# Column halves in the values' product, attention on the memory rows first, and a new order of steps, in a two-layer cross-attention kernel

## The chip, the cores and the metric

The kernel runs on one core of a Trainium2 chip, as one launch. The metric is the device time of that launch in microseconds (us). TensorE (PE), VectorE (DVE), ScalarE (ACT), GpSimd (POOL) and SyncE (SP, which here only starts transfers) work side by side and wait for each other on semaphores. All data is float32. "PEld" is TensorE's loading of stationary operands, which the profile lists apart from its products.

## The reference, cut to what matters

There are 32 sequences of 64 tokens with 256 features. Layer 0 is an expert block: each token goes through one of two weight sets ("v" and "l"). Layer 1 attends to a memory of 64 rows with 128 features for each sequence.

```python
# layer 0 (16 heads; head width 16 in self-attention, 8 in cross-attention)
x = rms_norm(hidden, ln_in_w)
q, k, v = split(where(vm, x @ v_qkv, x @ l_qkv))
ctx = softmax(causal(rope(q) @ rope(k).T / 4)) @ v
hidden = hidden + where(vm, ctx @ v_dense, ctx @ l_dense)
ck, cv = split(encoder @ ckv_w)
cctx = softmax(rms_norm(hidden) @ cq_w @ ck.T / sqrt(8)) @ cv
hidden = hidden + cctx @ cdense_w
mi = rms_norm(hidden)
hidden = hidden + where(vm, silu(mi@v_gate)*(mi@v_up)@v_down, silu(mi@l_gate)*(mi@l_up)@l_down)

# layer 1 (one head, width 256; W_mem is 256 x 128)
memory_proj = memory @ W_mem.T
attn = softmax(hidden @ memory_proj.T / 16)
memory_context = attn @ memory_proj
gate = sigmoid(concat(hidden, memory_context) @ W_gate.T + b_gate)
out = rmsnorm(hidden + gate * memory_context) * norm_w
```

## The kernel before

The 2048 tokens are 16 tiles of 128 tokens; a tile holds two sequences (b = 0 and 1, 64 rows each). Two tiles (t = 0 and 1) make a group, and there are 8 groups. A tile goes through steps with names: `qkv`, `qkvv` (projections), `qkT` (turn queries and keys), `score_a`/`score` (scores), `probT` (turn the exponentials), `pv` (weights times values), `ctxT`, `dense`, `h1T`, `cproj`, and then the same for cross-attention: `cscore_a`/`cscore`, `cprobT`, `cpv`, `cctxT`, `cdense`. The finished rows are scattered to DRAM in the order of their expert (`sort`). The third part, the expert MLP, works on 17 slots m of 128 sorted rows: `m_in`, `miT`, `gu0` to `gu2`, `hT0`, `hT1`, `down`, `m_out`. Layer 1 (section L1 of the order) gathers the rows back (`h3_in`) and runs `h3T`, `hw`, `mscore`, `attnT`, `gate`, `fuse`, `fin`, `store` for each of the 16 tiles, with four sets of buffers u.

The order in which each engine does its steps is written out by hand in a table `ORDER`, one list for each engine and section: W0 to W7 (a group of layer 0 each, from W1 on with MLP slots mixed in), MID (the rest of the MLP) and L1. `run` walks through the table. An engine never leaves this order, it only waits.

Precise products split both operands in a high and a low part (`split_product`, `x_product`). A plain float32 product of the kernel shows up in the trace as two matmul records, each with a weight load of its own; a turn (`transpose`) shows up as one.

Scores are computed in strips: the stationary operand is 32 rows by 64 columns, so that a quarter of the array's rows and half of its columns work on one strip, and four strips (`strip_scores`, line 1344) with different rows lie in the array side by side. The mask is put in by a product with 64 rows (line 1353). Everything else in layer 0 uses all 128 rows and columns.

The values' product is `apply` (line 1381), called by `pv` (hd = 16) and `cpv` (hd = 8). For each of 8 pairs of heads, the stationary operand is `pT[t][:, k, :]`: 128 rows (two heads by 64 keys) by 128 columns (two sequences by 64 queries). The moving operand holds the values of both sequences, 2 x 2 x (hd + 1) columns, 68 or 36 wide; the one more column gives the sum of the exponentials. So every query gets a result with the values of both sequences, and `normed` (lines 1034 and 1038, on DVE) reads only the half that belongs to it: two reciprocals and two multiplications, one for each sequence, each on 64 partitions.

In layer 1, `h3T` turns the tile's rows (line 1536) and computes `mp` = memory @ W_mem.T (line 1539, 256 columns); ACT copies both at once (line 786, 512 columns). `mscore` computes the scores (lines 1561 and 1562) and, into the other half of the bank, `mpg` = memory @ (W_gate2 @ W_mem).T (line 1563, 256 columns); ACT copies it (line 800) after the exponentials (line 799). `attnT` turns the weights (line 1569; copy in line 805), and `gate` multiplies them with `mp` (line 1574) and with `mpg` (line 1575).

## Time and profile before

| | us |
|---|---|
| median of 3 runs | 557.07 (554.66 to 559.98) |
| the profiled execution, its own time | 557.75 |
| its span, first to last instruction | 555.9 |
| busy in the span: PE / PEld / DVE | 482.8 / 389.9 / 380.2 |
| busy in the span: ACT / POOL | 252.5 / 150.5 |
| mean granted TensorE clock | 0.959 of full |

The busy times overlap, since engines work side by side. The span has four stretches: start and group W0 up to about 85 us, where weights are still loaded and split; six repeats of the same 50.3 us (W1 to W6) up to 386 us; W7 and MID up to about 465 us; and layer 1 from 470 us to the end. Between MID and layer 1 TensorE waits for rows that go to DRAM and come back.

### The profile page before, as it was taken

How to read it: one execution, taken by the hardware profiler on the slowest of the kernel's cores; microseconds unless marked ns; L12 is line 12 of the kernel's file. 1: busy time of each engine (PE TensorE's matmuls, PEld its weight loads, DVE VectorE, ACT ScalarE, POOL GpSimd, SP SyncE). 2: the span in 40 equal slices, each digit the busy share in tenths (PEclk: the TensorE clock that was granted, in tenths of full speed). 3: DMA queues.
4: the chain of work that ended last, by engine and by line, in shares of the span. 5: the costliest groups of instructions: out<-in, count | busy, mean ns of one | idle time of the engine just before them, and what ended most of it. 6: DMA issues, size and time to landing. Idle time of an engine off the chain costs nothing.

```text
span 555.9 us, 9884 instructions
## 1 busy us (share of the span) xinstructions
PE 482.8 (87%) x3462; PEld 389.9 (70%) x3462; DVE 380.2 (68%) x852; ACT 252.5 (45%) x694; POOL 150.5 (27%) x262
## 2 busy tenths in 40 slices
PE   0688887999999999999999999999997895988984
PEld 0566465677778777877878787777776784856762
DVE  4889978876885888588578858875875452245444
ACT  3256434444544445355354525443542331555663
POOL 6162221213031230303131221313011202254452
PEclk9978799999999999999999999999998798888998
DMA  6643500001011000101010110001000131021111
GB/s 202 186 132 102 171 10 20 11 29 58 2 39 47 22 11 28 59 11 39 11 58 2 40 47 21 19 20 50 1 11 22 36 106 47 11 75 54 43 58 38
DMA packets 22688, 27.07 MB, mean 49 GB/s; under 512 B 3280, under 2 KB 19408, under 8 KB 22640
## 3 DMA queue, kind: packets, MB, share of 16 engines
q1 hardware_dynamic: 20992, 22.08, 12.6%
q0 software_dynamic: 1648, 4.36, 2.6%
q8 instruction: 29, 0.48, 0.3%
q14 instruction: 19, 0.16, 0.1%
HBM read 19.74 MB, written 6.68 MB: 48 GB/s over the span
## 4 chain that ended last, share of the span: by engine, by line
PE 71%; DVE 16%; ACT 6%; DMA 3%; issue 3%; SPq 1%; POOL 1%; POOLq 0%; ACTq 0%
PE xyz L1318 8%; PE xyz L1344 7%; PE b_ps L1497 7%; PE xyz L1381 5%; PE xyz L1322 4%; PE xyz L1369 3%; DVE E L1018 3%; PE b_ps L1500 3%; DVE mx L1016 3%; PE xyz L1547 2%; PE b_ps L1289 2%; PE b_ps L1290 2%; PE b_ps L1291 2%; PE b_ps L1511 2%; ACT vb L685 2%
## 5 line engine op out<-in xcount | busy, mean ns | idle before, releaser
L1195 POOL TENSOR_TENSOR var<-ss,pow_eps 128x1 f32<-128x1 f32 x32 | 8.2, 256 | 247.7 <-ACT att L664 164.7
L1381 PEld LDWEIGHTS xyz<-vb,kT 128*128 128x128 f32 x512 | 62.1, 196 | 7.2 <-issue 5.4
L1381 PE MATMUL xyz<-vb,kT 128*128 128x36 f32 (+1 forms) x512 | 63.5, 280 | 1.5 <-DVE kT L1071 1.2
L1016 DVE TENSOR_REDUCE mx<-xyz 128x8 f32<-128x512 f32 x64 | 43.7, 683 | 11.5 <-PE xyz L1344 11.4
L1344 PE MATMUL xyz<-kT,qT 32*64 32x128 f32 (+1 forms) x768 | 44.4, 332 | 4.9 <-ACT qT L722 3.3
L1369 PE MATMUL xyz<-cst,E 128*128 128x128 f32 x256 | 39.2, 287 | 8.3 <-ACT E L695 5.6
L1018 DVE TENSOR_TENSOR E<-xyz,mx 128x512 f32<-128x512 f32 x64 | 44.2, 691 | 2.2
L1369 PEld LDWEIGHTS xyz<-cst,E 128*128 128x128 f32 x256 | 29.5, 146 | 14.9 <-ACT E L695 8.3
L1497 PE MATMUL b_ps<-w_gu_hi,ms_hi 128*128 (+2 forms) x90 | 37.4, 416 | 0.6 <-ACT ms_hi L752 0.6
L728 ACT ACTIVATE E<-E,rstd 128x512 f32<-128x512 f32 x32 | 23.1, 723 | 31.2 <-DVE E L1018 31.2
L1344 PEld LDWEIGHTS xyz<-kT,qT 32*64 32x64 f32 x768 | 21.0, 135 | 20.9 <-PE xyz L1344 8.4
L685 ACT ACTIVATE vb<-xyz,rstd 64x128 f32<-64x128 f32 x64 | 23.6, 369 | 26.5 <-PE xyz L1322 25.3
L1497 PE MATMUL b_ps<-w_gu_lo,ms_hi 128*128 (+2 forms) x90 | 34.1, 380 | 0.0
L695 ACT ACTIVATE E<-E 128x512 f32<-128x512 f32 x32 | 20.1, 628 | 28.6 <-DVE E L1018 28.6
L1289 PE MATMUL b_ps<-w_down_hi,hidT_hi 128*128 (+1 forms) x90 | 27.4, 304 | 1.2 <-DVE hidT_lo L1115 1.2
L764 ACT ACTIVATE th<-b_ps,mrh 128x256 f32<-128x256 f32 (+1 forms) x45 | 20.0, 444 | 17.5 <-PE b_ps L1500 17.3
L1500 PE MATMUL b_ps<-w_gu_hi,ms_lo 128*128 (+2 forms) x90 | 26.9, 381 | 0.0
L1318 PE MATMUL xyz<-w_qkv_hi,xs_vhi 128*128 128x512 f32 (+1 forms) x64 | 23.6, 380 | 2.9 <-issue 2.3
L1290 PE MATMUL b_ps<-w_down_lo,hidT_hi 128*128 (+1 forms) x90 | 26.2, 291 | 0.0
L1291 PE MATMUL b_ps<-w_down_hi,hidT_lo 128*128 (+1 forms) x90 | 26.1, 290 | 0.0
L1122 DVE TENSOR_TENSOR xm<-b_ps,xm 128x256 f32<-128x256 f32 x15 | 6.4, 425 | 27.7 <-PE b_ps L1291 27.6
L1097 DVE SCALAR_TENSOR_TENSOR th<-th,b_ps 128x256 f32<-128x256 f32 (+1 forms) x45 | 17.6, 391 | 10.5 <-ACT th L764 9.3
(268 smaller groups left out, 1305.0 us busy)
## 6 DMA issues: line engine op xcount, KB each, us to landing
xm<-h_rows SPq DMA_DIRECT2D x17, 128.0 KB, 2.1
h_rows<-xm SPq DMA_DIRECT2D x17, 128.0 KB, 1.7
xT<-in_xT_dram SPq DMA_DIRECT2D x8, 256.0 KB, 3.1
x_sb<-in_x_dram SPq DMA_DIRECT2D x8, 256.0 KB, 3.1
ctxT_a<-in_ctxT_dram SPq DMA_DIRECT2D x8, 128.0 KB, 2.3
over_xs<-in_ctxT_dram SPq DMA_DIRECT2D x4, 256.0 KB, 3.3
out_dram<-late SPq DMA_DIRECT2D x8, 128.0 KB, 1.7
out_dram<-over_qkv SPq DMA_DIRECT2D x8, 128.0 KB, 1.7
```

The costliest lines, as they stand in the source:

```text
L685: act.activation(vb[t][e * SEQ:(e + 1) * SEQ, b, :, e, 0:HD], v[rows, :, e, :], ACT.Copy, scale=rstd[rows, 0, t:t + 1]).then_inc(S["vb_rea ...
L1016: dve.tensor_reduce(mx[:, t, heads], s, AX.X, ALU.max).then_inc(max_ready, 1)
L1018: dve.tensor_tensor(E[t][:, b * 512:(b + 1) * 512].rearrange("p (h k) -> p h k", k=SEQ), s, mx[:, t, heads].unsqueeze(2).to_broadcast([P, ...
L1289: pe.matmul(o, sh, mh, start=start, stop=False)
L1290: pe.matmul(o, sh, ml, start=False, stop=False)
L1291: return pe.matmul(o, sl, mh, start=False, stop=stop)
L1318: pe.matmul(o, xs[e][0][:, c, cols], w_qkv[s][:, e, c, a:b], start=(e == 0 and c == 0 and s == 0), stop=False)
L1344: last = pe.matmul(xy[t][q, hp, o:o + w], qT[t][rows, c, q], kT[t][rows, (2 * c + b) * w:(2 * c + b + 1) * w], start=not masked, stop=True ...
L1369: last = pe.transpose(xy[t][:, a // 4, (a % 4) * P:(a % 4 + 1) * P], E[t][:, a * P:(a + 1) * P], ident)
L1381: last = pe.matmul(yz[t][:, a, 0:4 * (hd + 1)], pT[t][:, k, :], vb[t][:, :, a, :, HD - hd:HD + 1], start=True, stop=True)
L1497: pe.matmul(o, ms[m % 2][0][:, c, :], weights(s, c), start=(c == 0 and s == 0), stop=False)
L1500: last = pe.matmul(o, ms[m % 2][1][:, c, :], weights(0, c), start=False, stop=(c == HC - 1))
```

## The change: what it does

In `apply` each product is made twice, once for each sequence b: the stationary operand is 128 rows by the 64 columns of b's queries, the moving operand has b's values alone (34 or 18 columns), and the result goes to b's 64 partitions. So there are 16 products where there were 8, each with half of the array's columns. `normed` then reads one layout on all 128 partitions: one reciprocal and one multiplication.

In layer 1, `h3T` turns the memory rows instead of computing `mp`; ACT copies 384 columns. `mpg`, its product and its copy are gone. A new step `mix` multiplies the turned memory rows with the attention weights (128 columns), ACT copies the result (`mixT`), and `gate` is one product with `w_memT`, 512 columns wide, which gives both halves.

`inv_rms` counts on one semaphore instead of two, which frees the semaphores for `mix`. Its instructions stay.

```diff
             def apply(t, hd, done):
                 for k in range(PAIRS):
                     a = 4 * (k % 4 // 2) + 2 * (k // 4) + k % 2 if hd == HD else k
-                    last = pe.matmul(yz[t][:, a, 0:4 * (hd + 1)], pT[t][:, k, :], vb[t][:, :, a, :, HD - hd:HD + 1], start=True, stop=True)
+                    for b in range(2):
+                        q = slice(b * SEQ, (b + 1) * SEQ)
+                        last = pe.matmul(yz[t][q, a, 0:2 * (hd + 1)], pT[t][:, k, q], vb[t][:, b, a, :, HD - hd:HD + 1], start=True, stop=True)
                 last.then_inc(done, 1)
...
             def normed(n, t, hd, pv_ps, rec_ready, done):
-                for b in range(2):
-                    rows = slice(b * SEQ, (b + 1) * SEQ)
-                    dve.reciprocal(rec[rows, t, :]..., o[rows, b, :, :, hd]).then_inc(rec_ready, 1)
-                for b in range(2):
...
-                    dve.tensor_tensor(att[t][rows, 0:NH * hd]..., o[rows, b, :, :, 0:hd], ... ALU.mult).then_inc(done, 1)
+                dve.reciprocal(rec[:, t, :].rearrange("p (a e) -> p a e", e=2), o[:, :, :, hd]).then_inc(rec_ready, 1)
+                dve.wait_ge(rec_ready, tl(n, t))
+                dve.tensor_tensor(att[t][:, 0:NH * hd]..., o[:, :, :, 0:hd], ... ALU.mult).then_inc(done, 1)
...
             def h3T_(n, t):        # TensorE
-                pe.matmul(L[u][:, H:2 * H], memory(n, t), w_memT[:, 0:H], start=True, stop=True).then_inc(S["h3T_ps"], 1)
+                pe.transpose(L[u][:, H:H + P], memory(n, t), ident).then_inc(S["h3T_ps"], 1)
...
             def h3T_(n, t):        # ScalarE
-                act.activation(h3m[u], L[u], ACT.Copy).then_inc(S["h3T_ready"], 1)
+                act.activation(h3m[u][:, 0:H + P], L[u][:, 0:H + P], ACT.Copy).then_inc(S["h3T_ready"], 1)
...
             def mscore(n, t):      # TensorE, and its copy on ScalarE
-                pe.matmul(L[u][:, 0:P], hwT[u], memory(n, t), start=False, stop=True)
-                pe.matmul(L[u][:, H:2 * H], memory(n, t), w_memT[:, H:2 * H], start=True, stop=True).then_inc(S["ms_ps"], 1)
+                pe.matmul(L[u][:, 0:P], hwT[u], memory(n, t), start=False, stop=True).then_inc(S["ms_ps"], 1)
-                act.activation(mpg[u], L[u][:, H:2 * H], ACT.Copy).then_inc(S["mpg_ready"], 1)
...
+            def mix(n, t):         # TensorE
+                pe.wait_ge(S["mwT_ready"], tl(n, t))
+                pe.matmul(L[u][:, 0:P], mem[u], mwT[u], start=True, stop=True).then_inc(S["mix_ps"], 1)
+            def mix(n, t):         # ScalarE
+                act.wait_ge(S["mix_ps"], tl(n, t))
+                act.activation(mixT[u], L[u][:, 0:P], ACT.Copy).then_inc(S["mix_ready"], 1)
             def gate(n, t):
-                pe.matmul(L[u][:, 0:H], mwT[u], mp[u], start=True, stop=True)
-                pe.matmul(L[u][:, H:2 * H], mwT[u], mpg[u], start=True, stop=True).then_inc(S["gate_ps"], 1)
+                pe.wait_ge(S["mix_ready"], tl(n, t))
+                pe.matmul(L[u], mixT[u], w_memT[:, :], start=True, stop=True).then_inc(S["gate_ps"], 1)
...
             ("W2", dict(           # the table ORDER, TensorE's list, one of all that are new
-                    miT:1 qkT:4 qkT:5 score_a:4 score:4 gu0:1 gu1:1 score_a:5 probT:4 score:5 gu2:1 pv:4 probT:5
+                    qkT:4 miT:1 qkT:5 score_a:4 score:4 gu0:1 gu1:1 score_a:5 probT:4 score:5 gu2:1 hT0:1 pv:4 probT:5
```

The table is new in every section. Three places show what that means. The first is TensorE in W2, from the values' product of tile 4 (`pv:4`) to that of tile 5; the name `kT` stands for `pT`, which shares its buffer. Before:

```order
L1381 MATMUL xyz<-vb,kT 128x68 x8
L1369 MATMUL xyz<-cst,E 128x128 x8
L1392 MATMUL xyz<-cst,att 128x128 x2
L1398 MATMUL xyz<-ctxT_a,w_ckv 128x128
L1399 MATMUL xyz<-w_ckv,ctxT_a 128x128
L1511 MATMUL b_ps<-cst,hid 128x128 x6
L1289 MATMUL xyz<-w_dense_hi,attT_hi 128x512
L1290 MATMUL xyz<-w_dense_lo,attT_hi 128x512
L1291 MATMUL xyz<-w_dense_hi,attT_lo 128x512
```

And after the change:

```order
L1514 MATMUL b_ps<-cst,hid 128x128 x4
L1384 MATMUL xyz<-vb,kT 64x34 x16
L1370 MATMUL xyz<-cst,E 128x128 x8
L1514 MATMUL b_ps<-cst,hid 128x128 x2
L1395 MATMUL xyz<-cst,att 128x128 x2
L1401 MATMUL xyz<-ctxT_a,w_ckv 128x128
L1402 MATMUL xyz<-w_ckv,ctxT_a 128x128
L1384 MATMUL xyz<-vb,kT 64x34 x16
```

The eight products are sixteen of half the size; two of the six turns of `hid` stand between the exponentials' turns and those of `att`; and `pv:5` follows `ctxT:4` at once, where `dense:4` stood between them before. The second place is DVE around the same two products. Before:

```order
L1034 RECIPROCAL rec<-xyz 64x16 x2
L1038 TENSOR_TENSOR att<-xyz,rec 64x256 x2
L1055 TENSOR_TENSOR attT_lo<-xyz,attT_hi 128x256
L247 TENSOR_TENSOR kT<-xyz,cst 128x512
L1026 COPY kT<-xyz 128x512
L1047 SCALAR_TENSOR_TENSOR h_0<-xyz,route_t,x_sb 128x256
L1050 SCALAR_TENSOR_TENSOR h_0<-xyz,route_t,h_0 128x256
```

And after the change:

```order
L1037 RECIPROCAL rec<-xyz 128x16
L1039 TENSOR_TENSOR att<-xyz,rec 128x256
L1031 COPY kT<-xyz 128x512
L1056 TENSOR_TENSOR attT_lo<-xyz,attT_hi 128x256
L247 TENSOR_TENSOR kT<-xyz,cst 128x512
L1037 RECIPROCAL rec<-xyz 128x16
L1039 TENSOR_TENSOR att<-xyz,rec 128x256
```

Each pair of instructions is one, and the second tile's copy and division come ahead of the first tile's residual sum. The third place is TensorE in layer 1, near the end, where the steps of several tiles alternate. Before:

```order
L1536 MATMUL xyz<-cst,over_qkv 128x128 x2
L1539 MATMUL xyz<-w_memT,over_xs 128x256
L1561 MATMUL xyz<-block_h,ident_h 128x128
L1562 MATMUL xyz<-over_xs,over_qkv 128x128
L1563 MATMUL xyz<-w_memT,over_xs 128x256
L1574 MATMUL xyz<-late 128x256
L1575 MATMUL xyz<-late 128x256
```

And after the change (1539 and 1542 are `h3T`, 1564 and 1565 `mscore`, 1575 `gate`, 1580 `mix`):

```order
L1575 MATMUL xyz<-w_memT,late 128x512
L1539 MATMUL xyz<-cst,over_qkv 128x128 x2
L1542 MATMUL xyz<-cst,over_xs 128x128
L1564 MATMUL xyz<-block_h,ident_h 128x128
L1565 MATMUL xyz<-over_xs,late 128x128
L1548 MATMUL xyz<-over_qkv,w_mem 128x128 x2
L1550 MATMUL xyz<-w_gate,over_qkv 128x256 x2
```

The two products with `w_memT` and 256 columns are gone from their places, a turn stands for the first, and the 512 columns are made at once in `gate`.

## Rows read from the trace of the kernel before

**Rows 1.** Busy time in stretches: length, then PE, PEld, DVE, ACT, POOL, clock, DMA.

```profile
0.00:84.80 84.80, 57.07 (x353) 43.26 (x354) 66.66 (x139) 36.50 (x78) 31.35 (x55) 0.90 0.43 132
135.10:185.40 50.30, 48.14 (x385) 39.73 (x384) 38.14 (x83) 23.33 (x63) 11.70 (x20) 1.00 0.10 30
470.00:545.00 75.00, 67.39 (x341) 52.69 (x342) 32.42 (x99) 43.03 (x148) 34.32 (x55) 0.91 0.16 48
```

**Rows 2.** The chain that ended last, by engine.

```profile
PE 71%; DVE 16%; ACT 6%; DMA 3%; issue 3%; SPq 1%; POOL 1%; POOLq 0%; ACTq 0%
```

**Rows 3.** PE in order of time (start, length, count): `pv`, turns of `cprobT`, `cpv`.

```profile
199.91 1.90 PE L1381 MATMUL xyz<-vb,kT 128*128 128x68 f32 x16
201.64 0.39 PE L1415 MATMUL xyz<-cst,h 128*128 128x128 f32 x2
...
211.81 1.04 PE L1369 MATMUL xyz<-cst,E 128*128 128x128 f32 x8
212.68 0.61 PE L1423 MATMUL xyz<-qT,w_cq 128*128 128x128 f32 x4
...
215.00 1.97 PE L1381 MATMUL xyz<-vb,kT 128*128 128x36 f32 x16
216.81 0.41 PE L1497 MATMUL b_ps<-w_gu_hi,ms_hi 128*128 x1
```

**Rows 4.** PEld, the loads of one `cscore` from 205.30 on: one, four, five.

```profile
205.30 0.13 PEld L1344 LDWEIGHTS xyz<-kT,qT 32*64 32x64 f32 x1
205.30 0.15 PEld L1344 LDWEIGHTS xyz<-kT,qT 32*64 32x64 f32 x4
205.30 0.19 PEld L1344 LDWEIGHTS xyz<-kT,qT 32*64 32x64 f32 x5
```

**Rows 5.** PEld by line and shape: count, busy us, mean ns, idle before.

```profile
L1381 PEld LDWEIGHTS xyz<-vb,kT 128*128 128x128 f32 x512 | 62.1, 196 | 7.2 <-issue 5.4 <-ACT kT L733 1.1
L1369 PEld LDWEIGHTS xyz<-cst,E 128*128 128x128 f32 x256 | 29.5, 146 | 14.9 <-ACT E L695 8.3 <-ACT E L728 5.3 <-issue 1.0
```

**Rows 6.** The chain in layer 1 in order of time: start, length, what.

```profile
482.57 0.45 PE xyz L1545 x4
...
518.29 0.43 PE xyz L1539 x2
...
519.06 0.43 PE xyz L1563 x2
...
523.82 0.43 PE xyz L1574 x2
```

**Rows 7.** PE in order of time around one half of the cross scores.

```profile
206.39 0.39 PE L1399 MATMUL xyz<-w_ckv,ctxT_a 128*128 128x128 f32 x2
206.71 0.66 PE L1344 MATMUL xyz<-kT,qT 32*64 32x256 f32 x8
207.30 0.50 PE L1497 MATMUL b_ps<-w_gu_hi,ms_hi 128*128 x1
207.64 0.40 PE L1497 MATMUL b_ps<-w_gu_lo,ms_hi 128*128 x1
```

**Rows 8.** DVE and PE by line and shape, around `normed`.

```profile
L1034 DVE RECIPROCAL rec<-xyz 64x16 f32<-64x16 f32 x64 | 16.1, 252 | 2.6 <-PE xyz L1381 1.5
L1038 DVE TENSOR_TENSOR att<-xyz,rec 64x256 f32<-64x256 f32 x32 | 13.5, 422 | 1.0
L1038 DVE TENSOR_TENSOR att<-xyz,rec 64x128 f32<-64x128 f32 x32 | 9.2, 289 | 1.0
L1392 PE MATMUL xyz<-cst,att 128*128 128x128 f32 x32 | 7.0, 301 | 2.4 <-DVE att L1038 2.1
```

**Rows 9.** ACT by line and shape in layer 1.

```profile
L786 ACT ACTIVATE late<-xyz 128x512 f32<-128x512 f32 x8 | 4.8, 596 | 12.5 <-PE xyz L1539 12.3
L791 ACT ACTIVATE late<-xyz 128x128 f32<-128x128 f32 x8 | 2.2, 278 | 6.1 <-PE xyz L1547 6.1
L800 ACT ACTIVATE late<-xyz 128x256 f32<-128x256 f32 x8 | 3.0, 377 | 0.0
```

More of the change, by code:

```diff
@@ L181, in xattn_kernel @@
         h3T = [h3m[u][:, 0:H].rearrange("p (c q) -> p c q", c=HC) for u in range(NB)]
-        mp = [h3m[u][:, H:2 * H] for u in range(NB)]
-        mpg = [late_piece(u, 3 * H, 4 * H) for u in range(NB)]
+        mem = [h3m[u][:, H:H + P] for u in range(NB)]
+        mixT = [h3m[u][:, H + P:H + 2 * P] for u in range(NB)]
         mw = [late_piece(u, 4 * H, 4 * H + P) for u in range(NB)]
@@ L366, in xattn_kernel @@
+                    cprobT:2 hT1:0 cscore:3 down:0 cpv:2 cprobT:3 cctxT:2 cdense:2 cpv:3 qkv:4 cctxT:3 cdense:3 qkvv:4
+                    qkv:5 qkvv:5""",
             )),
@@ L385, in xattn_kernel @@
+                    cscore:4 gu2:2 hT0:2 cproj:5 cscore_a:5 cprobT:4 hT1:2 cscore:5 down:2 cpv:4 cprobT:5 cctxT:4
+                    cdense:4 cpv:5 qkv:6 cctxT:5 cdense:5 qkvv:6 qkv:7 qkvv:7""",
             )),
@@ L404, in xattn_kernel @@
+                    cscore:6 gu2:4 hT0:4 cproj:7 cscore_a:7 cprobT:6 hT1:4 cscore:7 down:4 cpv:6 cprobT:7 cctxT:6
+                    cdense:6 cpv:7 qkv:8 cctxT:7 cdense:7 qkvv:8 qkv:9 qkvv:9""",
             )),
@@ L423, in xattn_kernel @@
+                    cscore:8 gu2:6 hT0:6 cproj:9 cscore_a:9 cprobT:8 hT1:6 cscore:9 down:6 cpv:8 cprobT:9 cctxT:8
+                    cdense:8 cpv:9 qkv:10 cctxT:9 cdense:9 qkvv:10 qkv:11 qkvv:11""",
             )),
@@ new lines, in xattn_kernel @@
+                    probT:11 hT1:7 ctxT:10 miT:8 ctxT:11 h1T:10 gu0:8 dense:10 cproj:10 gu1:8 h1T:11 dense:11 gu2:8
+                    hT0:8 cproj:11 cscore:10 cprobT:10 hT1:8 cscore:11 cprobT:11 cctxT:10 xsq:12 cctxT:11 xsq:13
+                    rope:12 rope:13""",
+                dve="""
+                    qkT:10 miT:7 qkT:11 score:10 gu0:7 gu1:7 probT:10 score:11 gu2:7 pv:10 probT:11 hT1:7 hT0:7
+                    ctxT:10 pv:11 miT:8 down:7 dense:10 ctxT:11 xsplit:12 dense:11 gu0:8 gu1:8 cscore:10 gu2:8 hT0:8
+                    cprobT:10 hT1:8 cscore:11 cpv:10 cprobT:11 cdense:10 cpv:11 xsq:12 down:8 cdense:11 xsq:13 rope:12
+                    rope:13""",
@@ L457, in xattn_kernel @@
-                    cscore:13 cpv:12 gu2:10 cprobT:13 hT0:10 cdense:12 hT1:10 xsq:14 cpv:13 down:10 cdense:13 xsq:15
-                    rope:14 rope:15""",
+                    qkT:12 miT:9 qkT:13 score:12 gu0:9 gu1:9 probT:12 score:13 gu2:9 pv:12 probT:13 hT1:9 hT0:9
+                    ctxT:12 pv:13 miT:10 down:9 dense:12 ctxT:13 xsplit:14 dense:13 gu0:10 gu1:10 cscore:12 gu2:10
+                    hT0:10 cprobT:12 hT1:10 cscore:13 cpv:12 cprobT:13 cdense:12 cpv:13 xsq:14 down:10 cdense:13
@@ new lines, in xattn_kernel @@
+                    mix:1 fuse:0 hw:3 attnT:2 gate:1 mscore:3 mix:2 fuse:1 attnT:3 mix:3 gate:2 h3T:4 fuse:2 hw:4
+                    gate:3 mscore:4 h3T:5 attnT:4 fuse:3 mix:4 hw:5 h3T:6 mscore:5 gate:4 attnT:5 hw:6 mix:5 fuse:4
+                    mscore:6 h3T:7 attnT:6 gate:5 hw:7 mix:6 fuse:5 mscore:7 attnT:7 gate:6 mix:7 fuse:6 h3T:8 gate:7
+                    hw:8 fuse:7 h3T:9 mscore:8 hw:9 attnT:8 mix:8 h3T:10 mscore:9 attnT:9 gate:8 hw:10 h3T:11 fuse:8
+                    mix:9 mscore:10 attnT:10 hw:11 mix:10 gate:9 mscore:11 attnT:11 fuse:9 gate:10 mix:11 h3T:12
@@ new lines, in xattn_kernel @@
+                    mix:1 hw:3 gate:1 attnT:2 mscore:3 mix:2 attnT:3 gate:2 mix:3 h3T:4 gate:3 hw:4 mscore:4 h3T:5
+                    attnT:4 hw:5 mix:4 h3T:6 gate:4 mscore:5 hw:6 attnT:5 mix:5 mscore:6 h3T:7 gate:5 attnT:6 hw:7
+                    mix:6 mscore:7 gate:6 attnT:7 h3T:8 mix:7 gate:7 hw:8 h3T:9 mscore:8 hw:9 attnT:8 h3T:10 mix:8
+                    mscore:9 gate:8 attnT:9 hw:10 h3T:11 mscore:10 mix:9 hw:11 attnT:10 gate:9 mix:10 mscore:11
+                    gate:10 attnT:11 mix:11 h3T:12 gate:11 hw:12 mscore:12 attnT:12 h3T:13 mix:12 hw:13 gate:12 h3T:14
@@ L539, in xattn_kernel @@
+                    mscore:13 hw:14 attnT:13 h3T:15 mscore:14 mix:13 hw:15 attnT:14 gate:13 mix:14 mscore:15 gate:14
+                    attnT:15 mix:15 gate:15""",
             )),
@@ L1224, in xsq @@
                     pool.wait_ge(S["vb_ready"], 4 * (tl(n, t) - 2))
-                inv_rms(0, t, n, S["ssx"], S["r1v"], S["r1"])
+                inv_rms(0, t, n, S["ssx"], S["r1"])
             def rope_add(n, t):
@@ L1233, in dense @@
             def dense(n, t):
-                inv_rms(1, t, n, S["ss1"], S["r2v"], S["r2"])
+                inv_rms(1, t, n, S["ss1"], S["r2"])
             def m_sq(n, t):
@@ L1389, in ctxT @@
             def ctxT(n, t):
-                pe.wait_ge(S["att_ready"], half(n, t, 1))
+                pe.wait_ge(S["att_ready"], tl(n, t))
                 for c in range(HC):
```

277 lines of the change are left out of this document (124 added, 153 removed).

## The prediction

> **What bounds the kernel now.** I read the stretches first. In a repeat of 50.30 us TensorE works 48.14 us at the full granted clock (1.00, which is 2.4 GHz), DVE 38.14 us, ACT 23.33 us [rows 1]. There are six such repeats, and 71% of the chain that ended last is PE [rows 2]. So TensorE's own time sets the pace from 85 to 386 us, and what it saves there comes off the end. Two stretches are less clear: up to 84.80 us DVE works 66.66 us and TensorE 57.07 us, and in layer 1 (470 to 545 us) TensorE works 67.39 of 75.00 us at a mean clock of 0.91, so that a tenth of it is waiting [rows 1].
>
> **The values' product.** Then I read how long one `apply` occupies TensorE: from its first record to the next step's first. That is 1.73 us for `pv` (199.91 to 201.64) and 1.81 us for `cpv` (215.00 to 216.81), 16 records each, 0.11 us a record [rows 3]. The moving operand is 68 columns in one and 36 in the other, and the record costs the same; so it isn't the moving columns that are paid for but the load of 128 stationary columns. I take 1.77 us as the mean of the two. There are 512 records, which is 32 such products.
>
> After the change there are 32 records, each with 64 stationary columns. What a load of 64 columns costs is seen in the strips: four loads of four different strips are over 0.02 us after one alone would be, and the fifth, the second of the first strip, 0.06 us later than the first, call it 0.055 [rows 4]. So 64 columns take half of what 128 take, and parts of the array that don't overlap load at the same time. But the four strips lie in different rows. The two halves of the new product use the same 128 rows and different columns, and no row of this trace shows such a pair. The bounds are these:
> - both halves load side by side: 16 pairs of 0.055, 0.88 us;
> - one load at a time: 32 of 0.055, 1.76 us;
> - one load at a time, and none while the other half's product streams: see the third rival.
>
> I take the first. The rows nearest to it are the strips [rows 4], and a second one speaks for it: the load of a turned operand, also 128x128 float32, lasts 146 ns where the product's lasts 196 ns [rows 5]. The way from memory to the array thus delivers the same data faster than an ordinary load asks for, and two half loads at once needn't wait for it.
>
> The Trainium skill is of two minds here. "TensorEngine Tiling (Array Packing)", section Key Properties, says that different tiles of the array can load and multiply in parallel; by that the product would take the 0.88 us. "TensorE: Matmul & The Clock Gate", section "The mechanism", says that a load overlaps with a running product only when its rows differ; by that it would be the third rival. The trace speaks against that second sentence at least for the whole array: at 0.11 us a record, the load of the same rows must already run beside the stream.
>
> **Leaving one shape of the array for another** costs TensorE time, and the change adds such places. A float32 product of 256 moving columns streams for 0.215 us a record [rows 6], so one of 128 for 0.11. Before the strips, the two records from 206.39 on would let the next begin at 206.61; the strips begin at 206.71, and stream only after their first load (0.055), so going in costs 0.15. The strips have streamed by 206.71 + 0.055 + 0.43 + 0.02 = 207.21; the next record starts at 207.30 and lasts 0.50 instead of 0.40, so going out costs 0.19 [rows 7]. Together 0.34 us. All but one of the 32 products now stand between full-array steps, so each pays it: 0.88 + 0.34 = 1.22 us against 1.77, a saving of 0.55. With 28 of them in W1 to W7 that is 15.4 us; the four of W0, where DVE is the busier engine [rows 1], I count at half, 1.1. Of these 16.5 us I take 10% off, because TensorE will catch up with engines that hide behind it now: **-14.9 us**. The scores' halves are also parted more often than before (52 ways out of the strips instead of 45), which is free: two halves in a row wait for each other about as long as a way out and in takes.
>
> **DVE around it.** Each product had two reciprocals (252 ns) and two multiplications (422 or 289 ns), and has one of each [rows 8]; a DVE instruction on 128 partitions costs what one on 64 does, as all of its work goes by columns. This removes 32 x 0.252 + 16 x 0.422 + 16 x 0.289 = 19.4 us of DVE's 380, of which most lies beside TensorE. On the path is what TensorE waits for: 2.4 us before the turns of `att` in `ctxT` [rows 8], and the answer now comes 0.67 us earlier. I take **-1.5 us**, between 0 and -3.
>
> **Layer 1.** TensorE per tile, at the full clock. Removed: `mp` (0.43), `mpg` (0.43), and the two products of `gate` (0.43 each) [rows 6], 1.72 us. Added: one turn, 0.11 (eight take 0.87 from 211.81 to 212.68 [rows 3]); `mix`, two records of 128 columns, 0.22 (four take 0.45 [rows 6]); the 512 columns, twice 0.43. That is 1.19, a saving of 0.53 us, or 8.5 us for 16 tiles. ACT per tile: the copy of 512 columns (0.596) becomes one of 384, between 0.377 and 0.596, about 0.49; the copy of `mpg` (0.377) goes and one of 128 columns (0.278) comes [rows 9], -0.2 us. The chain of one tile gets a product and a copy longer (about 0.4 + 0.3 with the hand-over) and loses `mpg` ahead of the row maximum (0.43) and its copy ahead of the turn (0.38), so it stays as long. TensorE is busy 90% of this stretch [rows 1], so most of the saving should show: three quarters, **-6.4 us** (between -2 and -9). The change of `inv_rms` moves a count and no work: 0.
>
> **The order.** Every engine's list is new; in the steps I compared, TensorE gets MLP work in front of a step that waits, and the second tile's product earlier. TensorE's idle time in a repeat is 50.30 - 48.14 = 2.2 us [rows 1], so a better order can give at most about 1.5 us a repeat, and a worse one costs as easily. I count 0, with +-4 us over all.
>
> **Sum.** -14.9 - 1.5 - 6.4 = -22.8 us. The profiled execution took 557.75 us, 1.85 more than its span of 555.9; it becomes 535.0. It lies 0.7 us above the median of the three runs, 557.07, which becomes 534.3. I say **535**, and 527 to 543 if this case holds.
>
> **Rival 1: the saving turns into waits.** The halves load side by side, but TensorE then waits for DVE and ACT, whose chain through a tile (maximum, subtraction, exponential, copy) isn't shorter except by 0.67 us. For it: 16% of the chain that ended last is DVE [rows 2]. Against it: DVE needs 38.14 - 2.4 = 35.7 us of a repeat and has room. Half of the 14.9 us would go: 543 to 551, about 546.
>
> **Rival 2: one load at a time.** Both halves fetch weights from the same partitions, and if these can serve one load only, a pair takes 0.11 us, and the product 1.76 + 0.34 = 2.10 us, 0.33 more than before: +10.6 us for 32. With -1.5 and -6.4 that is +2.7, about 560 (555 to 566). The change breaks even when a pair takes 0.105 us, so this case is near no change. For it: no row shows two loads into the same rows at once. Against it: the faster load of the turned operand [rows 5].
>
> **Rival 3: slower.** A half loads only when the other half's stream has ended. The stream of 34 columns is 0.215 x 34/256 = 0.028 us, of 18 columns 0.015. `pv` takes 32 x 0.083 + 0.34 = 3.0 us (+1.27), `cpv` 32 x 0.070 + 0.34 = 2.58 us (+0.77), for 16 of each +32.6 us; with the other terms +24.7, about 582. It decides from a pair of 0.105 us on, and would be at 0.14 to 0.17. For it: twice as many instructions on the busiest engine. Against it: in the strips the second load of a strip starts 0.055 us after the first, while the first product streams [rows 4, 7].
>
> There is also a small chance that changing to column halves costs nothing, as its loads are of full height: 11 us less, about 524.
>
> **How the numbers follow.** My case 0.50, rival 1 0.13, rival 2 0.22, rival 3 0.12, the last 0.03. A measurement of this kernel can tell about 1% (5.6 us) from no change. Faster by more (below 551.5): 0.50 + 0.13 + 0.03, less a little of rival 1's end, 0.65. Within 1% (to 562.6): most of rival 2, 0.17. Slower: the rest of it and rival 3, 0.18. The range for 8 in 10 takes my case, rival 1 and rival 2: 527 to 566.
>
> **What the new profile would show.** If I'm right: the distance from the first record of a values' product to the next step's is 1.2 us instead of 1.8, with loads starting in pairs every 0.055 us; a repeat lasts about 48 us; DVE's busy time is near 361 us; TensorE in layer 1 works some 8 us less, and the stretch from 470 to 545 is about 6 us shorter. If that distance is 2.1 us, rival 2 holds, at 2.6 to 3.0 us rival 3. If it is 1.2 us and the repeat still lasts over 49 us, rival 1. What would make all of it wrong is an order that lets TensorE wait longer somewhere than before, which would show as idle time before one step in every repeat.

## The result, and the profile after

The changed kernel took 535.13 us (median of 4 runs, 533.81 to 538.41), and the kernel before, run again beside it, 555.89 us (4 runs, 554.66 to 559.98). The ratio is 0.962, with a 95% interval from 0.955 to 0.969: faster by about 21 us. The profiled execution took 534.4 us, with a span of 532.6 us, 23.3 less than before.

Busy time in three stretches of the changed kernel: a repeat at the place of the one shown before, another one from the first product of one group's mask (`causal_h`, line 1354) to that of the next group's, and layer 1 from its first turn of `h3` to about its last product. The columns are those of [rows 1].

```profile
130.00:178.00 48.00, 45.31 (x445) 36.00 (x444) 35.87 (x75) 22.99 (x63) 11.66 (x20) 1.00 0.10 32
180.10:228.41 48.31, 45.71 (x448) 36.42 (x448) 36.24 (x75) 23.34 (x64) 11.90 (x21) 1.00 0.10 32
451.66:525.00 73.34, 62.84 (x303) 43.32 (x304) 36.12 (x106) 41.29 (x155) 35.40 (x58) 0.94 0.16 51
```

The same two stretches, cut at the same products, in the kernel before:

```profile
185.34:235.61 50.27, 48.13 (x384) 39.71 (x384) 38.15 (x83) 23.33 (x63) 11.69 (x20) 1.00 0.09 30
470.29:549.00 78.71, 69.78 (x352) 54.19 (x352) 35.29 (x107) 45.38 (x156) 35.79 (x58) 0.92 0.16 49
```

A repeat is 1.96 us shorter. TensorE works 2.42 us less in it, so it waits 2.60 us instead of 2.14. With such cuts the 23.3 us lie as follows: 1.8 before the second group, 11.2 in the six repeats, 5.6 in W7 and the rest of the MLP, 4.8 in layer 1. The six are not quite the same: the first lasts 48.1 us before and 46.6 after, the five others 50.3 and 48.3. Of the 5.6 us in W7 and the MLP, the four products explain 2.8 (4 x 0.69); the same stretch is 4.6 us shorter in e2 and 3.1 in e4, so what the order has in it isn't settled. DVE works 364.9 us in all instead of 380.2. The chain that ended last, by engine, beside [rows 2]:

```profile
PE 61%; DVE 18%; ACT 9%; issue 6%; DMA 4%; POOL 1%; SPq 1%; POOLq 0%; ACTq 0%
```

PE in order of time around a `pv` and a `cpv`, to be read beside [rows 3]:

```profile
192.52 1.13 PE L1384 MATMUL xyz<-vb,kT 128*64 128x34 f32 x32
193.64 0.41 PE L1472 MATMUL b_ps<-cst,xm 128*128 128x128 f32 x2
...
214.85 0.70 PE L1451 MATMUL xyz<-w_cdense,qT 128*128 128x256 f32 x2 [0.37 <-ACT qT L738]
215.49 1.11 PE L1384 MATMUL xyz<-vb,kT 128*64 128x18 f32 x32
216.53 0.51 PE L1319 MATMUL xyz<-w_qkv_hi,xs_vhi 128*128 128x512 f32 x1
```

From the product's first record to the next step's it is 1.12 and 1.04 us, where it was 1.73 and 1.81. (The repeat's other `cpv` takes 1.04 too; after its first `pv` the next step waits 0.45 us for exponentials, and the distance is 1.57.) The loads of the first of the two show why:

```profile
192.49 1.04 PEld L1384 LDWEIGHTS xyz<-vb,kT 128*64 128x64 f32 x32 [0.15 <-issue]
```

There are 32 loads in 1.04 us and one of them lasts 0.14, so they start 0.90/31 = 0.029 us apart: a pair, one load for each half of the columns, takes 0.058 us. The halves load side by side; e5 below tests it.

Where TensorE waits in that repeat (in all, times, longest, in us):

```profile
PE xyz L1334 <- ACT vb L686: 0.8, 1, 0.8
PE xyz L1451 <- ACT qT L738: 0.7, 2, 0.4
PE xyz L1370 <- ACT E L696: 0.4, 1, 0.4
PE xyz L1345 <- ACT qT L723: 0.4, 1, 0.4
```

The wait in front of the turns of `att` is not on this list. DVE and PE by line and shape, beside [rows 8]:

```profile
L1037 DVE RECIPROCAL rec<-xyz 128x16 f32<-128x16 f32 x32 | 8.1, 253 | 8.7 <-PE xyz L1384 8.7
L1039 DVE TENSOR_TENSOR att<-xyz,rec 128x256 f32<-128x256 f32 x16 | 6.8, 425 | 0.6
L1039 DVE TENSOR_TENSOR att<-xyz,rec 128x128 f32<-128x128 f32 x16 | 4.7, 292 | 0.6
L1395 PE MATMUL xyz<-cst,att 128*128 128x128 f32 x32 | 6.7, 294 | 3.7 <-DVE att L1039 3.7
```

Half as many instructions, each as long as before: 128 partitions cost what 64 did (253 against 252 ns). The turns' wait of 3.7 us is a single one in W0, at 44.0 us.

By these rows DVE saves the 19.4 us that the prediction had, but its busy time fell by 15.3 only. Another instruction of DVE, a subtraction in `xsplit`, got longer in the new order (before, then after):

```profile
L967 DVE TENSOR_TENSOR xs_lhi<-xs_lhi,xs_vhi 128x512 fp32r<-128x512 f32 x8 | 6.4, 796 | 0.3
L972 DVE TENSOR_TENSOR xs_lhi<-xs_lhi,xs_vhi 128x512 fp32r<-128x512 f32 x8 | 12.3, 1531 | 0.3
```

It takes 1.52 to 1.54 us wherever POOL runs its two operations on `xs_llo` at the same time, all eight times after and once before, and 0.69 us the other seven times before. This is 0.84 us of DVE's time in every repeat; whether it delays TensorE was not tested.

Two of layer 1's rows, beside [rows 9]: ACT's copy of 384 columns, which had been estimated, and `gate`'s one product.

```profile
L787 ACT ACTIVATE over_qkv<-xyz 128x384 f32<-128x384 f32 x8 | 3.9, 493 | 1.3 <-PE xyz L1542 1.3
L1575 PE MATMUL xyz<-w_memT,late 128*128 128x512 f32 x16 | 9.2, 662 | 0.1
```

### The profile page after: what moved, and what is told of

It is laid out like the page before. It is cut to its first block, busy times and chain, and to the rows that moved or that the text cites. A ratio compares the mean times of both kernels' runs of the same rounds, so it can differ in the third digit from the quotient of the medians.

```text
span 532.6 us, 10731 instructions
## 1 busy us (share of the span) xinstructions
PE 450.1 (85%) x3926; PEld 350.9 (66%) x3926; DVE 364.9 (69%) x788; ACT 249.0 (47%) x694; POOL 152.4 (29%) x262
## 4 chain that ended last, share of the span: by engine, by line
PE 61%; DVE 18%; ACT 9%; issue 6%; DMA 4%; POOL 1%; SPq 1%; POOLq 0%; ACTq 0%
PE xyz L1319 9%; PE xyz L1370 5%; PE b_ps L1500 5%; PE xyz L1345 5%; PE xyz L1384 4%; PE xyz L1323 4%; DVE E L1023 3%; DVE mx L1021 3%; PE xyz L1550 3%; PE b_ps L1290 2%; PE xyz L1575 2%; PE b_ps L1503 2%; ACT vb L686 2%; PE xyz L1451 2%; PE b_ps L1291 2%
## 5 line engine op out<-in xcount | busy, mean ns | idle before, releaser
L1345 PE MATMUL xyz<-kT,qT 32*64 32x128 f32 (+1 forms) x768 | 42.4, 320 | 4.0 <-ACT qT L723 3.2
L1370 PEld LDWEIGHTS xyz<-cst,E 128*128 128x128 f32 x256 | 28.3, 144 | 18.8 <-ACT E L696 9.2
L1255 POOL DMA_INDIRECT h_rows<-h,slot_i x16 | 16.7, 1044 | 79.3 <-DVE h L1081 75.6
L1384 PEld LDWEIGHTS xyz<-vb,kT 128*64 128x64 f32 x1024 | 33.2, 139 | 8.8 <-issue 6.4
L1384 PE MATMUL xyz<-vb,kT 128*64 128x18 f32 (+1 forms) x1024 | 36.3, 220 | 2.3 <-DVE kT L1031 1.2
L1207 POOL TENSOR_TENSOR xs_vlo<-xs_llo,route 128x512 fp32r<-128x512 f32 x8 | 12.7, 1591 | 75.4 <-DVE xs_llo L981 75.4
L1345 PEld LDWEIGHTS xyz<-kT,qT 32*64 32x64 f32 x768 | 20.2, 130 | 17.6 <-issue 9.7
L711 ACT ACTIVATE vb<-xyz 64x64 f32<-64x64 f32 x64 | 14.3, 223 | 25.0 <-DVE kT L247 23.8
L241 POOL TENSOR_TENSOR qk<-E 128x256 f32<-128x256 f32 x16 | 14.3, 893 | 38.0 <-DVE E L1003 38.0
```

Source lines behind the costliest of these rows:

```text
L1345: last = pe.matmul(xy[t][q, hp, o:o + w], qT[t][rows, c, q], kT[t][rows, (2 * c + b) * w:(2 * c + b + 1) * w], start=not masked, stop=True ...
L1370: last = pe.transpose(xy[t][:, a // 4, (a % 4) * P:(a % 4 + 1) * P], E[t][:, a * P:(a + 1) * P], ident)
L1384: last = pe.matmul(yz[t][q, a, 0:2 * (hd + 1)], pT[t][:, k, q], vb[t][:, b, a, :, HD - hd:HD + 1], start=True, stop=True)
```

## The experiments

Ratios are to runs of the kernel before that were made beside them on the same chip, with 95% intervals. Different experiments ran on different chips, so ratios are compared, not times; 0.01 is 5.6 us. A repeat's length is taken between the first mask products of two groups, as above, where TensorE's granted clock stayed full.

**e1_full_width**: the changed kernel with the values' product and `normed` of before.

```diff
-                    for b in range(2):
-                        q = slice(b * SEQ, (b + 1) * SEQ)
-                        last = pe.matmul(yz[t][q, a, 0:2 * (hd + 1)], pT[t][:, k, q], vb[t][:, b, a, :, HD - hd:HD + 1], start=True, stop=True)
+                    last = pe.matmul(yz[t][:, a, 0:4 * (hd + 1)], pT[t][:, k, :], vb[t][:, :, a, :, HD - hd:HD + 1], start=True, stop=True)
```

> The changed kernel with the values' product and the division after it as they were (8 products with 128 stationary columns, two reciprocals and two multiplications), everything else of the change kept: the new layer 1 and the new order. If the column halves carry what I booked on them (14.9 us for TensorE and 1.5 for DVE), this takes 16 us more than the changed kernel, about 551 us. Rival, the new order carries the middle and the halves little: it stays under 541 us.

Measured: 559.9 us (11 runs), ratio 1.005 [1.002, 1.009]. With layer 1 new and every list new, but the old product, the kernel is no faster than before. A repeat takes 51.07 us where TensorE's clock was full, 0.8 more than before, and nearly all of that is waiting (2.87 us instead of 2.14). The order brings two waits in front of the turns of `att`, for which the kernel before has a single one of 0.29 us (in all, times, longest, in us):

```profile
PE xyz L1397 <- DVE att L1043: 0.4, 1, 0.4
PE xyz L1449 <- DVE att L1043: 0.4, 1, 0.4
```

So the halves and the one division are worth 0.043, or 24 us, in this order, where I expected 16. The repeats at full clock make up 6 x 2.76 = 16.6 us of it. The kept trace is that of the longest of the 11 runs (566.32 us) and can't place the rest.

**e2_halves_alone**: the kernel before with the halves and the one division, in the order of before.

```diff
-                    last = pe.matmul(yz[t][:, a, 0:4 * (hd + 1)], pT[t][:, k, :], vb[t][:, :, a, :, HD - hd:HD + 1], start=True, stop=True)
+                    for b in range(2):
+                        q = slice(b * SEQ, (b + 1) * SEQ)
+                        last = pe.matmul(yz[t][q, a, 0:2 * (hd + 1)], pT[t][:, k, q], vb[t][:, b, a, :, HD - hd:HD + 1], start=True, stop=True)
```

> The kernel before with the column halves and the single reciprocal and multiplication alone, old order, old layer 1. By the booking 16.4 us less than before: about 539.5 us. If the halves gain only in the order that was searched for them, 545 us or more.

Measured: 544.87 us (4 runs), ratio 0.981 [0.973, 0.988], so 10.8 us. One repeat of it, and TensorE's waits in that repeat:

```profile
180.05:229.05 49.00, 45.63 (x449) 36.44 (x446) 35.61 (x76) 23.34 (x63) 11.61 (x21) 1.00 0.10 31
```

```profile
181.35 0.41 PE L1329 MATMUL xyz<-cst,qk 128*128 128x128 f32 x2 [0.80 <-ACT vb L685]
...
192.44 0.65 PE L1365 MATMUL xyz<-cst,E 128*128 128x128 f32 x4 [0.67 <-ACT E L695]
...
198.03 0.41 PE L1467 MATMUL b_ps<-cst,xm 128*128 128x128 f32 x2 [0.58 <-DVE hidT_lo L1111]
...
209.31 1.41 PE L1340 MATMUL xyz<-kT,qT 32*64 32x256 f32 x16 [0.37 <-ACT qT L722]
...
214.31 0.66 PE L1365 MATMUL xyz<-cst,E 128*128 128x128 f32 x4 [0.60 <-ACT E L728]
```

TensorE works 2.50 us less than before (48.13 to 45.63), but the repeat is only 1.27 shorter: its waiting grew from 2.14 to 3.37 us. In the kernel before, the three waits at the exponentials' turns and the MLP's next input were 0.15 to 0.19 us each; now they are 0.67, 0.60 and 0.58. Half of what the product saves comes back as waits for the exponentials and for `hidT_lo`.

**e3_layer1_alone**: the kernel before with the new layer 1 and its order, W0 to MID as before.

```diff
-                pe.matmul(L[u][:, H:2 * H], memory(n, t), w_memT[:, 0:H], start=True, stop=True).then_inc(S["h3T_ps"], 1)
+                pe.transpose(L[u][:, H:H + P], memory(n, t), ident).then_inc(S["h3T_ps"], 1)
...
-                pe.matmul(L[u][:, 0:H], mwT[u], mp[u], start=True, stop=True)
-                pe.matmul(L[u][:, H:2 * H], mwT[u], mpg[u], start=True, stop=True).then_inc(S["gate_ps"], 1)
+                pe.matmul(L[u], mixT[u], w_memT[:, :], start=True, stop=True).then_inc(S["gate_ps"], 1)
```

> The new layer 1 alone (its steps and its order), with the old values' product and the old order of all sections before. My term for it was -6.4 us (-2 to -9); the trace of the changed kernel has this stretch 4.8 us shorter. So 549.5 to 551 us. If the sum of this kernel's saving and that of the halves alone is under 18 us, a part of the gain belongs to the order.

Measured: 555.64 us (10 runs), ratio 0.997 [0.993, 1.001]. In its trace layer 1, from the first turn of `h3` to the end, takes 81.19 us instead of 85.65. All kernels with the new layer 1 take 79.7 to 81.2 us for it, both with the old one 85.6 and 85.7; so it is worth some 4.5 to 6 us, of which the timing of this kernel shows 1.7, with an interval up to 4.0. By the timings this and e2 add up to 12.5 of the 21 us: the rest comes with the new order, or is scatter of the timings.

**e4_old_order**: all edits of the change, but W0 to MID in the order of before. TensorE's list of W2 stands for all:

```diff
-                    qkT:4 miT:1 qkT:5 score_a:4 score:4 gu0:1 gu1:1 score_a:5 probT:4 score:5 gu2:1 hT0:1 pv:4 probT:5
+                    miT:1 qkT:4 qkT:5 score_a:4 score:4 gu0:1 gu1:1 score_a:5 probT:4 score:5 gu2:1 pv:4 probT:5
```

> The changed kernel, but with the order of before in all sections up to the end of the MLP (layer 1 keeps its new order, as it has a new step). I counted 0 +-4 us for the order. The trace of the changed kernel has W7 and MID 5.6 us shorter, of which the four products of W7 explain only 2.4, so I now expect that the order is worth about 3 us: 538 us. Rival, the order is worth nothing: 535 us; or it carries much of the gain: 543 us or more.

Measured: 541.85 us (4 runs), ratio 0.974 [0.967, 0.980], a repeat of 49.01 us. The new order takes that to 0.962 and 48.31 us: it is worth 6 us (between 1 and 12 by the two intervals) with the halves and the one division, and costs 5 us with neither (0.997 to 1.005, e3 to e1). Which of the two it needs is seen in e6 and e9.

**e5_b_outer**: the changed kernel with the two loops of the product exchanged: eight products of sequence 0, then eight of sequence 1.

```diff
-                for k in range(PAIRS):
-                    a = 4 * (k % 4 // 2) + 2 * (k // 4) + k % 2 if hd == HD else k
-                    for b in range(2):
-                        q = slice(b * SEQ, (b + 1) * SEQ)
+                for b in range(2):
+                    q = slice(b * SEQ, (b + 1) * SEQ)
+                    for k in range(PAIRS):
+                        a = 4 * (k % 4 // 2) + 2 * (k // 4) + k % 2 if hd == HD else k
```

> The changed kernel with the sixteen products in another order: first the eight of sequence 0, then the eight of sequence 1, so that halves that could load side by side are eight products apart. If TensorE starts work on the two halves of the array in the order of the program, loads follow each other at 0.055 us: the product takes 1.8 us instead of 1.04 from its first load to the next step's, and a repeat grows from 48.31 us by up to 3 us. Rival: each half works through a queue of its own, the order doesn't matter, and the repeat stays at 48.3 us.

Measured, in one run: 552.8 us, a repeat of 50.53 us. PE and PEld of one `cpv` of it in order of time:

```profile
221.50 1.83 PE L1384 MATMUL xyz<-vb,kT 128*64 128x18 f32 x32
223.26 0.51 PE L1319 MATMUL xyz<-w_qkv_hi,xs_vhi 128*128 128x512 f32 x1
```

```profile
221.49 1.73 PEld L1384 LDWEIGHTS xyz<-vb,kT 128*64 128x64 f32 x32 [0.33 <-issue]
```

The same 32 loads start (1.73 - 0.14)/31 = 0.051 us apart instead of 0.029, and the product takes 1.76 us, as the full width did. So a load of the same half waits for the one before it, a load of the other half doesn't. The whole gain hangs on the alternation.

**e6_dve_in_two**: the changed kernel with the division and multiplication in two again, one for each sequence.

```diff
-                dve.reciprocal(rec[:, t, :].rearrange("p (a e) -> p a e", e=2), o[:, :, :, hd]).then_inc(rec_ready, 1)
+                for b in range(2):
+                    rows = slice(b * SEQ, (b + 1) * SEQ)
+                    dve.reciprocal(rec[rows, t, :].rearrange("p (a e) -> p a e", e=2), o[rows, :, :, hd]).then_inc(rec_ready, 1)
...
-                pe.wait_ge(S["att_ready"], tl(n, t))
+                pe.wait_ge(S["att_ready"], half(n, t, 1))
```

> The changed kernel with the division as before, two reciprocals and two multiplications on 64 partitions each: 2.4 us more work for DVE in a repeat, 19.4 us over all. I booked 1.5 us for it: 0.2 to 0.3 us per repeat, total 536.5 to 537.5 us. Rival, TensorE waits for it each time, 0.67 or 0.54 us at four places: a repeat of 50 us or more, and about 550 us.

Measured: 545.48 us (4 runs), ratio 0.976 [0.970, 0.982], a repeat of 49.2 to 49.3 us, 0.96 more. PE in order of time has two new waits in a repeat:

```profile
197.49 0.44 PE L1399 MATMUL xyz<-cst,att 128*128 128x128 f32 x2 [0.36 <-DVE att L1043]
...
220.46 0.33 PE L1451 MATMUL xyz<-cst,att 128*128 128x128 f32 x1 [0.26 <-DVE att L1043]
```

They are 0.62 of the 0.96 us. The other 0.35 stands as busy time of TensorE (46.06 us for 45.71); what makes it longer stays open. DVE's one division is thus worth 0.96 us a repeat, and by the timing 7.5 us in all (between 2 and 13 by the two intervals), not 1.5. In the profiles, half of the difference lies before the second group: 90.2 us against 84.7 to 88.0 in the seven other kernels that have one division and this order in W0, so a part of the 7.5 may be scatter.

**e7_extra_mid** and **e8_extra_first**: the changed kernel with one more product on all 128 columns in each `apply`, which writes to columns that nothing reads: in the middle (e7, shown) or ahead of the loop (e8).

```diff
                     a = 4 * (k % 4 // 2) + 2 * (k // 4) + k % 2 if hd == HD else k
+                    if k == 4:
+                        pe.matmul(yz[t][:, 0, 64:64 + 2 * (hd + 1)], pT[t][:, 0, :], vb[t][:, 0, 0, :, HD - hd:HD + 1], start=True, stop=True)
```

> The changed kernel with one more product of the full array (128 stationary columns, result to an unused place) in the middle of each values' product: its own two records, 0.22 us, and one more way in and out of the column halves. By my 0.34 us for that, 0.56 us each, 2.2 us in a repeat: 50.5 us. Rival, leaving the halves is cheap since their streams are short: 0.1 to 0.2 us each, a repeat of 49.6 to 50.0 us.

> The same extra product as in the run with it in the middle, but ahead of the halves, next to other full-array work: its own 0.22 us and no further change of shape, 0.9 us in a repeat, 49.2 us. What the other has more, divided by four, is the price of one way in and out.

Measured, one run each: 545.36 and 541.11 us, repeats of 49.76 and 48.93 us. PE in order of time, e7 and then e8:

```profile
196.54 0.66 PE L1386 MATMUL xyz<-vb,kT 128*64 128x34 f32 x16
197.13 0.41 PE L1383 MATMUL xyz<-vb,kT 128*128 128x34 f32 x2
197.47 0.66 PE L1386 MATMUL xyz<-vb,kT 128*64 128x34 f32 x16
198.25 0.41 PE L1474 MATMUL b_ps<-cst,xm 128*128 128x128 f32 x2
```

```profile
196.41 0.38 PE L1380 MATMUL xyz<-vb,kT 128*128 128x34 f32 x2
196.72 1.13 PE L1385 MATMUL xyz<-vb,kT 128*64 128x34 f32 x32
197.92 0.41 PE L1473 MATMUL b_ps<-cst,xm 128*128 128x128 f32 x2
```

The same work takes 1.71 us with the full product in the middle and 1.51 with it ahead. The one difference is one more way out of the column halves and in again: 0.20 us here, and 1.48 - 1.26 = 0.22 at the `cpv`. The repeats give (49.76 - 48.93)/4 = 0.21, but that is work less what waits took in: after a repeat's first `pv`, where the next step waits anyway, nothing of it shows (1.57 us in e7 as in the change). I had 0.34, from the strips.

**e9_old_order_dve_two**: e4 with e6's division in two, so that DVE's term is measured in the old order too. The diff is that of e6.

> The kernel with the halves and the new layer 1 in the old order of steps, and with the division and multiplication of the values' product in two again, one for each sequence. The same edit in the new order cost 7 to 10 us (0.96 us a repeat). Theory: it costs that much only because the new order lets TensorE come to the products' turns early; in the old order a step stands between them, so this kernel is 1 to 2 us slower than the old order with one division (0.9736 of the kernel before): ratio 0.975 to 0.978, a repeat of 49.0 to 49.3 us. Rival: DVE's shorter answer is worth the same in every order: ratio about 0.986, about 551 us, a repeat of 49.8 to 50.0 us.

Measured: 544.42 us (4 runs), ratio 0.974 [0.966, 0.982], the same as e4's 0.974; a repeat of 49.33 us, 0.32 more than e4's. As the theory had it: in the old order TensorE doesn't come to the turns of `att` early enough to wait for them (its waiting is 3.37 us in both; the 0.32 stand as busy time, 45.96 us for 45.63), and DVE's shorter answer is worth 2 us at most by the repeats, and nothing that the timing can tell. Beside e6 it shows more: with the halves and the division in two, the old order has 0.974 and the new one 0.976 (repeats of 49.33 and 49.27 us). So the new order gains nothing from the halves alone. What it is fitted to is the one division.

**e11_swaps**: the changed kernel with two swaps in TensorE's list in W1 to W7: `hT1` (two turns, 0.22 us) ahead of `probT` of the second tile and ahead of `cscore_a` of the second tile.

```diff
-                    qkT:4 miT:1 qkT:5 score_a:4 score:4 gu0:1 gu1:1 score_a:5 probT:4 score:5 gu2:1 hT0:1 pv:4 probT:5
-                    hT1:1 ctxT:4 pv:5
+                    qkT:4 miT:1 qkT:5 score_a:4 score:4 gu0:1 gu1:1 score_a:5 probT:4 score:5 gu2:1 hT0:1 pv:4 hT1:1 probT:5
+                    ctxT:4 pv:5
```

> Only the two swaps of TensorE's order out of the three edits. Theory: 0.4 us less of waiting a repeat, which lasts 47.9 us, and 532 us in all. Rival: the turns aren't in time there, or the steps that came before them now come later by as much (the exponentials' turns feed the values' product): a repeat of 48.3, 535 us.

Measured: 550.95 us (6 runs), ratio 0.987 [0.981, 0.994], 14 us slower than the change. Both theories fell. PE in order of time at the second swap, and DVE there:

```profile
210.34 0.44 PE L1493 MATMUL b_ps<-cst,hid 128*128 128x128 f32 x2 [1.73 <-DVE hid L1085]
210.70 0.71 PE L1324 MATMUL xyz<-kT,qT 32*64 32x256 f32 x8
211.35 1.97 PE L1349 MATMUL xyz<-cst,E 128*128 128x128 f32 x8
```

```profile
206.87 0.68 DVE L1000 TENSOR_REDUCE mx<-xyz 128x8 f32<-128x512 f32 x1
...
209.88 0.40 DVE L1085 SCALAR_TENSOR_TENSOR hid<-th,mrr,b_ps 128x176 f32<-128x176 f32 x1
```

The turns need `hid`, which DVE makes after the maxima and subtractions of the cross scores: it is ready at 210.28. The scores, which had to wait 0.41 us, now wait 1.73 behind the turns; at the first swap it is 0.85 us in place of 0.45. I had looked at how long the turns take and not at when their input comes.

**e10_three_waits**: the two swaps, and DVE makes two of the eight copies of a group's values, for which TensorE waits 0.80 us on ACT.

```diff
-                for b in range(2):
+                for b in range(2 - t):
...
+                if t == 1:
+                    dve.wait_ge(S["v_ps"], tl(n, t))
...
+                    for e in range(2):
+                        dve.tensor_scalar(vb[t][e * SEQ:(e + 1) * SEQ, 1, :, e, 0:HD], v[rows, :, e, :],
+                                          rstd[rows, 0, t:t + 1], None, ALU.mult).then_inc(S["vbd"], 1)
```

> The changed kernel with three edits at the three longest waits of TensorE in a repeat: the second half of the MLP's turns stands before the turns of the second tile's exponentials (0.45 us of waiting there) and before the cross scores of the second tile (0.41 us), with 0.22 us of turns to fill each, and DVE makes two of the eight copies of the values that TensorE waits 0.80 us for on ACT. Theory that these waits are the rest that is to be had: 0.2 + 0.2 + 0.5 us a repeat, which lasts 47.3 to 47.5 us instead of 48.3, and the whole is 6 us shorter, about 529, 0.99 of the changed kernel. Rival: another engine's chain stands behind each wait and takes its place, or DVE, which the halves' product waits for too, gets later by its two copies (2 x 0.25 us): a repeat of 48.3 to 48.8, the whole at 535 to 539.

Measured: 552.35 us (6 runs), ratio 0.985 [0.977, 0.993]. The swaps decide here too. Its undisturbed repeats last 49.74 us against 50.11 in e11, so the copies gain 0.37 us of a hoped-for 0.5.

**e12_dve_copies**: the changed kernel with the copies alone (the diff of e10), in its own order.

> The changed kernel in its own order, with the third edit alone: DVE makes two of the eight copies of the values in a group, for which TensorE waits 0.80 us on ACT once a repeat. With the two swaps this wait fell to 0.43 us and the repeat by 0.37 us (50.11 to 49.74 us where the clock held). Theory: the same without the swaps, a repeat of 47.9 to 48.0 us, 2 to 2.5 us less in all, about 533, a ratio to the kernel before of 0.956 to 0.960. Rival: in its own order DVE, busy 36 of 48 us, delays the first scores by its two copies and TensorE waits there instead: a repeat of 48.3 to 48.6, 535 to 537.

Measured: 535.78 us (6 runs), ratio 0.960 [0.956, 0.965], beside the change's 0.962 [0.955, 0.969]. Its repeats last 47.93 to 48.00 us where the change's last 48.31, as the theory had it, and the wait fell to:

```profile
185.05 0.41 PE L1345 MATMUL xyz<-cst,qk 128*128 128x128 f32 x2 [0.43 <-DVE vb L1012]
```

That is 1.9 us over five repeats, a third of what the timing can tell; whether this kernel beats the change stays open.

## Why the prediction was right, and where it was right by luck

The total was right: 535 predicted, 535.1 measured, and the profiled execution came down by 23.4 us where the sum had 22.8. Of the signs that it named, the repeat (48.3 us for "about 48") and the pairs of loads (0.058 us for 0.055) came as said; a product's distance fell further (1.04 to 1.12 us for 1.2), DVE's busy time less far (364.9 us for 361), and layer 1 gained less (4.8 us for 6). So the terms were not all right, and it was luck that their errors offset each other. These are the ratios that take it apart, each to the kernel before, and behind them a repeat's length in us at full clock:

| product and division | old order, old layer 1 | old order, new layer 1 | new order, new layer 1 |
|---|---|---|---|
| full width, division in two | 1; 50.27 | 0.997; 50.27 (e3) | 1.005; 51.07 (e1) |
| halves, division in two | | 0.974; 49.33 (e9) | 0.976; 49.27 (e6) |
| halves, one division | 0.981; 49.00 (e2) | 0.974; 49.01 (e4) | 0.962; 48.31 (the change) |

**The values' product.** The choice between the three bounds was right and is shown: a pair of loads takes 0.058 us, for 0.055 [rows 4]. Way in and out costs 0.21 us, not 0.34, so a product takes 1.08 us (the mean of 1.12 and 1.04), not 1.22, and saves 0.69, not 0.55. With that 32 products save TensorE 22 us, where my 0.55 gave 17.6. What then shows at the end was mis-sized the other way: I took 10% off for waits. In the old order half of a repeat's saving turned into waits (e2: 2.50 us less work, 1.27 us shorter). The term as put, -14.9 us, came out at -10.8 for it and the division together in the old order (e2), -13 with the new layer 1 (e3 to e4), and -16.5 for the product alone in the new order (e1 to e6). A repeat's share of the term, 4 x 0.55 less 10%, is 2.0 us; the product alone gives 0.94 in the old order (e3 to e9) and 1.80 in the new one (e1 to e6).

**DVE around it.** -1.5 us (0 to -3) holds in the old order (e9 to e4: 0.3 us a repeat) and was too small in the new one (e6 to the change: 0.96 us a repeat, 7.5 us in all by the timing, with 2 to 13 as its bounds). I read the price from the waits of the kernel before [rows 8], in an order that wasn't to stay. It is the order that makes DVE's answer late, not TensorE's faster product: with the full width e1 has both waits (0.38 and 0.37 us), and e9, with the halves in the old order, has neither.

**Layer 1.** -6.4 us predicted, 4.8 in the profiles. TensorE's work in the stretch fell by 6.94 us, not 8.5, and its waiting grew from 8.93 to 10.50 us. The prediction had the chain through a tile as long as before. TensorE's largest waits on ACT in that stretch, in the kernel before (lines 800 and 805 are the copies of `mpg` and of the turned weights):

```profile
PE xyz L1569 <- ACT over_qkv L800: 5.0, 5, 1.9
PE xyz L1574 <- ACT over_qkv L805: 2.2, 6, 0.4
```

And after (lines 795, 800, 805 and 810 are `hw`'s second copy, the exponentials, and the copies of the turned weights and of `mix`):

```profile
PE xyz L1564 <- ACT late L795: 1.9, 3, 0.7
PE xyz L1570 <- ACT late L800: 1.8, 2, 1.3
PE xyz L1580 <- ACT over_qkv L805: 1.3, 3, 0.5
PE xyz L1564 <- ACT over_qkv L795: 1.2, 3, 0.5
PE xyz L1575 <- ACT over_qkv L810: 1.0, 3, 0.4
```

The large wait behind the copy of `mpg` is gone, and many small ones stand at every hand-over of the longer chain: gained ahead of the turns, given back behind `hw` and `mix`. I did not separate why the work fell by less than the sum of the records.

**The order.** I counted 0 with +-4 us. It is -6 with the halves and the one division, nothing that the timing can tell with the halves alone (e9 to e6), and +5 with neither. "At most about 1.5 us a repeat" from TensorE's idle time of 2.2 us was a bound for the kernel before; once e2's waits stand in a repeat (3.37 us), there was more to win. The order, the division and the halves are not three terms that add up: what one is worth depends on the others, and the sum was right since the part that was lost to waits in one term was won back in another.

**The rivals.** Rival 1, the saving turns into waits, is what happens in the old order: 544.9 and 541.9 us (e2, e4), where it had about 546. I gave it 0.13 and spoke against it from DVE's share of busy time (38.14 of 50.30 us); the waits, though, are at ACT's exponentials and at single places in DVE's list, and a mean says nothing about these. In the changed kernel the new order and the one division together take most of it away (2.60 us of waiting in a repeat; 3.2 in e6, 3.37 in e2). Rivals 2 and 3 fell with the distance of the loads. The Trainium skill, "TensorE: Matmul & The Clock Gate", section "The mechanism", has a load overlap with a running product only when the rows differ; here the rows are the same, the columns differ, and 32 loads with their products take 1.04 us. The measurement decides for the other page of the Trainium skill, "TensorEngine Tiling (Array Packing)", section Key Properties, by which different tiles of the array load and multiply in parallel.

## What to carry to other kernels

Where the load of the stationary operand is what a product costs, and half of its result is thrown away, cut it into column halves and alternate between them instruction by instruction; keep each such run in one piece, since the way out and in costs 0.2 us. Price a saving on the busiest engine in the order that will stand in the end: in the old order half of it was lost, and the new order gained nothing with the division in two and was worse than the old one with the full width besides. Before moving a step into a wait, look up when its input is ready, not only how long it takes: a swap that was to fill 0.4 us of waiting made 1.7 us.
